# A scan kernel with its stores of y issued by SP in place of ACT, and the copies of C spread over three units

## The reference, cut to what matters

```
def step(state, inp):
    d, b, c, uu = inp
    dA = jnp.exp(d[..., None] * A_neg[:, None, :, :])
    state = dA * state + (d * uu)[..., None] * b[:, :, None, :]
    y = jnp.einsum('kbcn,kbn->kbc', state, c)
    return (state, y)
```

## Time and profile before

| | |
|---|---|
| median of 3 runs | 16748.27 us (16746.03 to 16751.82) |
| the profiled execution | 16740.79 us |
| its span | 16739.1 us |
| scan pass of layer 2 in it | about 8542 to 15095 us |
| granted clock of TensorE, mean | 0.856 |

### The profile page before, as it was taken

The page is one execution under the profiler, slowest core; times in us unless marked ns, Lnnn a source line. Parts: engine busy times, 40 slices in busy tenths (PEclk is TensorE's granted clock), DMA queues, the critical chain, the costliest instruction groups (busy, mean ns, idle before and its releaser), DMA issues. The chain is left out here.

```text
span 16739.1 us, 371849 instructions
## 1 busy us (share of the span) xinstructions
PE 13258.6 (79%) x130080; PEld 8791.3 (53%) x130080; DVE 11153.8 (67%) x10439; ACT 8476.8 (51%) x15113; POOL 6761.1 (40%) x3199
## 2 busy tenths in 40 slices
PE   7889999899988965444657887888778878887799
PEld 5666666666666642221235555555455545554477
DVE  5666666666666655554568887888788878885532
ACT  4444444444444435445556666666666666662200
POOL 1000000000000003234368888888888888881100
PEclk9999999999999988776768888888888888886799
DMA  5222222222222226668599999999999998997611
GB/s 128 58 68 57 57 60 55 61 60 56 58 65 61 55 86 159 157 163 201 147 210 208 207 208 206 206 208 208 206 207 208 207 205 207 208 209 211 184 44 37
DMA packets 1861415, 2344.84 MB, mean 140 GB/s; under 512 B 1067492, under 2 KB 1757932, under 8 KB 1836012
## 3 DMA queue, kind: packets, MB, share of 16 engines
q1 hardware_dynamic: 1606124, 2120.92, 53.4%
q10 hardware_dynamic: 242816, 134.91, 4.0%
q0 software_dynamic: 12288, 86.71, 2.3%
HBM read 1814.60 MB, written 556.32 MB: 142 GB/s over the span
## 5 line engine op out<-in xcount | busy, mean ns | idle before, releaser
L1789 DVE TENSOR_TENSOR_SCAN L2.h<-L2.ps,L2.db 128x912 f32<-128x912 f32 x2688 | 5400.7, 2046 | 1181.3 <-ACT L2.db L1712 1068.1
L1601 POOL TENSOR_TENSOR L2.db<-L2.du,L2.bt 128x896 f32<-128x896 f32 x2688 | 5560.1, 2097 | 1068.7 <-ACT L2.du L1719 832.6
L1623 PE MATMUL L2.ps<-L2.dm,L2.wa 32*128 32x112 f32 x21504 | 2441.9, 326 | 503.4 <-DVE L2.h L1789 383.7
L1705 ACT ACTIVATE L2.ps<-L2.ps 128x896 f32<-128x896 f32 x2688 | 2440.9, 908 | 492.0 <-PE L2.ps L1623 440.3
L1645 PE MATMUL L2.ps<-L2.h,L2.cd 128*8 128x96 f32 x50176 | 2576.8, 362 | 79.9 <-ACT L2.ysum L1726 67.1
L1623 PEld LDWEIGHTS L2.ps<-L2.dm,L2.wa 32*128 32x128 f32 x21504 | 1898.5, 220 | 1306.4 <-DVE L2.h L1789 785.6
L1635 PE MATMUL L2.ps<-L2.few,L2.fan 8*128 8x448 f32 x2688 | 1603.3, 680 | 832.9 <-ACT L2.du L1719 826.7
L1645 PEld LDWEIGHTS L2.ps<-L2.h,L2.cd 128*8 128x8 f32 x50176 | 1435.6, 108 | 806.3 <-ACT L2.ysum L1726 236.1
L1726 ACT COPY L2.ysum<-L2.ps 128x384 f32<-128x384 f32 x1568 | 751.7, 479 | 771.1 <-PE L2.ps L1645 666.5
L314 POOL TENSOR_TENSOR L1.x_res<-L1.x_res,L1.ob 96x3136 f32 (+1 forms) x16 | 95.4, 5977 | 2583.9 <-ACT L1.qv L457 2583.9
L1635 PEld LDWEIGHTS L2.ps<-L2.few,L2.fan 8*128 8x128 f32 x2688 | 443.5, 205 | 1192.4 <-ACT L2.du L1719 861.7
(11 more groups left out here) (258 smaller groups left out, 21196.1 us busy)
## 6 DMA issues: line engine op xcount, KB each, us to landing
L2.du<-du SPq DMA_DIRECT2D x4032, 224.0 KB, 6.0
L2.dm<-d SPq DMA_DIRECT2D x896, 336.0 KB, 7.2
y<-L2.ysum ACTq DMA_DIRECT2D x896, 84.0 KB
L0.left<-table SPq DMA_DIRECT2D x48, 1176.0 KB
L0.right<-table SPq DMA_DIRECT2D x48, 1176.0 KB
L1.left<-table SPq DMA_DIRECT2D x48, 1176.0 KB
L1.right<-table SPq DMA_DIRECT2D x48, 1176.0 KB
du<-L2p.work SPq DMA_DIRECT2D x64, 784.0 KB, 7.8
```

Of the source, the lines that this page charges most:

```text
L1601: pool.tensor_tensor(db[:, n % RB, :, 2:ROW], du[:, n % RD, :].rearrange("p (c t) -> p c t", t=SPAN), row, ALU.mult)\
L1623: mm = pe.matmul(decays[n % RA][:, lo:lo + SPAN], wa[rows, u * QUAD + e, :], dm[rows, u * QUAD + e, :], start=True, stop=True)
L1705: act.activation(a, a, ACT.Exp).then_inc(a_ready, 1)
L1789: dve.tensor_tensor_scan(h[:, half, u * UNIT:(u + 1) * UNIT, :].rearrange("p c t -> p (c t)"), decays[n % RA], db[:, n % RB, :, :].rearran ...
```

## The change

The four stores of a half-span's sums are no longer issued by ACT at the end of the half-span in which they are taken. SP issues them in the half-span after that: two in its unit 5 and two in its unit 6, behind the du loads of the same unit. At its unit 5 SP waits for `sum_out`, the count of takes, first. The wait of ACT at the first take, for `y_stored[half]`, keeps its place and its count; the counts of the semaphore come from the same four stores. After the last half-span SP stores the last two halves. The eight copies of C are made in lots of 3, 3 and 2 after units 11, 12 and 13 in place of all eight after unit 11 and the stores; their two waits stand before the first lot.

```
--- before.py
+++ after.py
@@ -1524,8 +1524,18 @@
                                   ap=[list(rows.ap[0]), [0, STATES // COPIES], list(rows.ap[1])])
                     sp.dma_start(du[:, slot, g * QUAD * SPAN:(g + 1) * QUAD * SPAN], src).then_inc(du_in[slot], 16)
 
-            def half_span(k, s, half, later, table):
-
+            def store_y(k, s, half, quarters):
+                for q in quarters:
+                    at = s * SPAN + SPAN // 4 * q
+                    if k % 2:
+                        at = at * -1 + (TOK - SPAN // 4)
+                    rows = slice(at, at + SPAN // 4) if isinstance(s, int) else bass.ds(at, SPAN // 4)
+                    place = y_dram[k, :, rows, half * HALF:(half + 1) * HALF]
+                    sp.dma_start(place, ysum[32 * q:32 * q + BATCH, :, :]).then_inc(y_stored[half], 16)
+
+            def half_span(k, s, half, earlier, later, table):
+
+                fills = count(sp, k, s, 2 * FILLS, (half - 1) * FILLS)
                 units = count(sp, k, s, 2 * UNITS, half * UNITS)
                 for u in range(UNITS):
                     sp.wait_ge(b_ready, units + (u + 1))
@@ -1541,6 +1551,11 @@
                             sp.wait_ge(cd_made, made)
                         steady(sp)
                         load_cc(k, s)
+                    if 5 <= u <= 6 and earlier is not None:
+                        if u == 5:
+                            sp.wait_ge(sum_out, fills + 2)
+                            steady(sp)
+                        store_y(*earlier, half, range(2 * (u - 5), 2 * (u - 5) + 2))
                     if u == 4 and table is not None:
                         sp.wait_ge(d_ready, count(sp, k, s, 4 * UNITS, half * 2 * UNITS))
                         load_wa(table, 1 - half)
@@ -1560,8 +1575,12 @@
                     later = (k + 1, 0) if k + 1 < DIRS else None
                 else:
                     later = (k, s + 1) if isinstance(s, int) else (k, sp.snap(s + 1))
-                half_span(k, s, 0, (k, s), k if k and isinstance(s, int) and s == 0 else None)
-                half_span(k, s, 1, later, k + 1 if last and k + 1 < DIRS else None)
+                if isinstance(s, int) and s == 0:
+                    earlier = (k - 1, NSPANS - 1) if k else None
+                else:
+                    earlier = (k, s - 1) if isinstance(s, int) else (k, sp.snap(s - 1))
+                half_span(k, s, 0, earlier, (k, s), k if k and isinstance(s, int) and s == 0 else None)
+                half_span(k, s, 1, earlier, later, k + 1 if last and k + 1 < DIRS else None)
 
             sp.wait_ge(cleared, 1)
             sp.dma_start(image[:], ap["c_image"]).then_inc(image_in, 16)
@@ -1576,6 +1595,9 @@
                 with sp.Fori(1, NSPANS - 1) as s:
                     span(k, s, False)
                 span(k, NSPANS - 1, True)
+            for half in range(2):
+                sp.wait_ge(sum_out, (DIRS * HALVES - 1 + half) * FILLS + 2)
+                store_y(DIRS - 1, NSPANS - 1, half, range(4))
             for half in range(2):
                 sp.wait_ge(y_stored[half], 64 * DIRS * NSPANS + 64)
 
@@ -1682,20 +1704,12 @@
             act.wait_ge(cleared, 1)
             act.wait_ge(image_in, 32)
 
-            def store_y(k, s, half):
-                for q in range(4):
-                    at = s * SPAN + SPAN // 4 * q
-                    if k % 2:
-                        at = at * -1 + (TOK - SPAN // 4)
-                    rows = slice(at, at + SPAN // 4) if isinstance(s, int) else bass.ds(at, SPAN // 4)
-                    place = y_dram[k, :, rows, half * HALF:(half + 1) * HALF]
-                    act.dma_start(place, ysum[32 * q:32 * q + BATCH, :, :]).then_inc(y_stored[half], 16)
-
-            def make_cd(k, s, fills):
-
-                act.wait_ge(cc_in, count(act, k, s, 16, 16))
-                act.wait_ge(sum_ready, fills + 2 * FILLS)
-                for b in range(BATCH):
+            def make_cd(k, s, fills, batches):
+
+                if batches[0] == 0:
+                    act.wait_ge(cc_in, count(act, k, s, 16, 16))
+                    act.wait_ge(sum_ready, fills + FILLS)
+                for b in batches:
                     act.activation(cd[:, b, :], cc[:], ACT.Identity, scale=image[:, b:b + 1]).then_inc(cd_made, 1)
 
             def decay(n, spreads):
@@ -1744,17 +1758,9 @@
                         copy_du(n // 4, n % 4 - 1, units, copies)
                     decay(n, spreads)
                     carry(half, u, units, begun)
-                if not first:
-                    act.wait_ge(sum_out, before + (FILLS + 2))
-                    steady(act)
-                    if half:
-                        store_y(k, s, 0)
-                    elif begun:
-                        store_y(k - 1, NSPANS - 1, 1)
-                    else:
-                        store_y(k, act.snap(s - 1), 1)
-                if half == 0:
-                    make_cd(k, s, before)
+                    if UNITS - 1 <= n <= UNITS + 1:
+                        at = 3 * (n - UNITS + 1)
+                        make_cd(k, s, count(act, k, s, 2 * FILLS), range(at, min(at + 3, BATCH)))
 
             for k in range(DIRS):
                 half_span(k, 0, 0, k == 0, True)
@@ -1765,8 +1771,6 @@
             act.wait_ge(y_stored[0], 64 * DIRS * NSPANS + 64)
             for f in range(FILLS):
                 take_sum(DIRS - 1, 1, f, (DIRS * HALVES - 1) * FILLS)
-            act.wait_ge(sum_out, DIRS * HALVES * FILLS + 2)
-            store_y(DIRS - 1, NSPANS - 1, 1)
 
         @block.vector
         def _(dve):
```

## The result

The changed kernel takes 17,702.7 us (median of 4 runs, 17,687.7 to 17,722.5), the kernel before 16,749.9 (4 runs): ratio 1.057, 95% interval 1.0552 to 1.0588. It is 953 us slower; forecast were 1,055 us, within 517 to 1,704. The profiled execution has a span of 17,686.0 us.

What follows compares the result with a forecast made beforehand. No engine was full; ACT's order of work set the pace. Per span 2 x 14.5 - 20.58 = +8.4 us, with the clock +9.4, x 112 = +1055 on 16,748.3: 17,800 us, between 17,265 and 18,450.

Steps and rivals of the forecast that it cites:

- take 0: First of seven copies from PSUM into ysum, in unit 4; ACT forecast to wait there some 220 times, 2 to 7 us.
- D: Stretch from Pool 11 to take 0, while SP issues and lands stores; 14.5 us a half, 12.6 to 17.
- the edit on the copies: Copies of C in lots over units 11 to 13, in time for the first sum in unit 15; costed at nothing.
- take 6: Last of the seven copies into ysum, unit 10; stretch from take 0 forecast within a microsecond of 14.5 and 15.5.
- Pool 11: End of GpSimd's unit 11 of a half, for which SP waits at its units 4 and 5.
- The issues ahead of the stores: SP's bt, dm and du issues and wait on sum_out between Pool 11 and the first store: 3.6 us.
- The two du loads in series: Unit 6's loads between second and third store, taken in series with the stores in SP's queue: 1.8 us.
- the lower bound 12.6: Least D: 3.6 us of issues ahead plus 9.0 us for the four stores nearly alone.
- The clock: TensorE idling before take 0 carries the low clock into the chain of sums: 1.0 us a span, 0 to 1.8.
- The first, stores landing in time: Rival: stores land before ACT needs them, decided at D = 10.3 us; faster, 16,130 us; chance 0.06.
- the second rival: Stores wait behind loads in SP's queue, SP issues du loads of units 8 to 10 late: 18,900 us; chance 0.08.
- ACT's relief: ACT freed of issuing the stores; claimed to be covered by the wait at take 0 and to bring nothing.

Runs made afterwards that it cites:

- e3: The changed kernel with all four stores in SP's unit 5, no du loads between them: 17,306.0 us.
- e11: The changed kernel, still one ysum, with SP's stores one each in units 5, 6, 7 and 8: 17,868.5 us.
- e4: The changed kernel with all four stores in SP's unit 4, behind its du loads and ahead of bt and dm: 16,873.6 us.
- e5: The changed kernel with two ysum, one for each half, SP's order of issues kept: 16,519.8 us.
- e2: The changed kernel with all eight copies of C after unit 11 instead of in lots: 17,710.5 us.
- e1: The kernel before with the copies of C in lots of 3, 3, 2, stores staying on ACT: 16,582.6 us.
- e6: Against the kernel before: two ysum, copies in lots, stores on ACT, one after each of units 0 to 3 of the next half: 16,181.0 us.
- e9: The kernel before with a second ysum and nothing else: 16,716.9 us.

## Why the prediction was right

**The mechanism.** It held at each step that the profile was to show: 222 waits at take 0 (220 forecast), no idle at unit 12, one of 4.6 us before unit 4, D alike in both halves (13.9 in the mean), no second wait for du in this kernel (GpSimd waits 106 us for du in the pass after, 212 before, by its waits), and the edit on the copies hidden. Cutting the span at take 0, take 6 and Pool 11 made it a sum of chains, and the change touched one of them directly. Two signs failed. Take 0 to take 6 stayed within a microsecond of its old time in half 1 (15.0 us in the mean, 14.5 before) but not in half 0 (17.0, 15.6 before). And SP's stores are not held 1 to 2 us each: their issue takes 0.30 us in the median, and the time shows at the loads behind them.

**D.** Predicted 14.5, measured 13.9 a half (27.8 / 2). The issues ahead of the stores were right to 0.1 us. The two du loads in series cost 1.4 us a half (e3 against the changed kernel) and not 1.8; the lower bound 12.6 was met by e3, which has no loads between, with 24.9 / 2 = 12.5. Against before that is +6.6 us a span by the means, in place of +8.4. Of the difference 0.6 is that the mean of before is 21.2, while the one span that I read had 20.58.

**The clock.** Predicted 1.0 us a span, measured +2.0 in take 0 to take 6 (32.0 against 30.0). That term was too small, since I counted one slow unit a half. In the span shown it is three in half 0: at 11018 to 11022 the granted clock is 0.50, 1.2 GHz, and the spread matmuls take 1.10 us (timeline of TensorE, after); by 11028 they are back at 0.65. In half 1 of the same span the clock is back at 1.00 by 11055, 4 us after take 0.

```profile
11025.65 1.10 PE L1645 MATMUL L2.ps<-L2.dm,L2.wa 32*128 32x112 f32 x8
...
11028.26 0.65 PE L1645 MATMUL L2.ps<-L2.dm,L2.wa 32*128 32x112 f32 x8
```

The spread of the spans agrees with that (65.0 to 68.6 us, 5 to 95% of them, with D varying by under 1 us). The trace also separates the clock from the wait before it. Take the 110 stretches take 0 to take 6 of half 0 (half-spans 3 to 222) and sort them by their mean granted clock; the last column is the longest idle of TensorE in the 12 us up to take 0:

```
granted clock    stretches   take 0 to take 6   D ahead   TensorE idle ahead
0.90 to 0.97        44            15.5 us        13.7 us        5.7 us
0.75 to 0.90        17            17.5           14.7           6.7
under 0.75          49            18.2           13.8           5.9
```

The first and the last row have nearly the same wait, yet the first takes no longer than before (15.6) and the last 2.6 us more. So the wait alone costs nothing behind take 0; the low clock does. e11 says the same: its wait is longer (D 15.3), its clock in these stretches higher (0.90 against 0.84), and take 0 to take 6 only 0.7 us above before. Why the clock comes back early in some spans and late in others stays open.

**The sum.** +6.6 + 2.0 = 8.5 us a span by unrounded values (forecast 9.4), x 112 = 952 against 953 measured. That these agree is no test, since the columns cover the whole span. That the forecast came within 102 us is in part luck: the D part was 1.8 us a span too high and the clock 1.0 too low, and these offset each other.

**The rivals.** The first, stores landing in time, was refuted. Its point of decision, D = 10.3, was right for the wait alone, and incomplete: e4 has D = 9.4 and is still slower, for the loads behind its stores. In this the second rival was half right: SP, held by the stores, does issue the loads behind them late. In the changed kernel those of units 8 to 10 are issued 6.6 to 7.1 us after their slot is free (1.8 to 4.1 before), but they still land 3.9 to 5.1 us ahead of their use, because VectorE is stopped at unit 4; GpSimd pays for it where loads are issued later still (e3, those of unit 6 at 6.3 us in place of 2.5) and where VectorE is hardly stopped or not at all (e4, e5). I had also written that ACT's relief is covered by the wait; in the changed kernel the lots are (e2). Outside it they are worth 167 us (e1), and with the stores apart some 400 more (e1 to e6, in which the second ysum, nearly nothing in e9, has its share in letting them be apart).

## What to carry to other kernels

When a store is moved to another issuer, look first at who reuses its source, and measure from the earliest moment at which the new issuer may issue to that reuse; with one buffer, four stores begun some 5 us later (3.5 after Pool 11 in place of 1.6 before) cost 953 us, with two buffers the same change won 230, and with one store a unit 570 (against e9, which has two buffers and the old order, 197 and 537). Put stores like these apart in a queue, since a row of four was paid by whatever was issued next, on either engine; no run varies their size or their rows. A part that gains alone may gain nothing in company (the lots: 167 us, 0 and 0 in three settings), so time each edit where it is to stand.

## What the runs showed of the hardware that was not expected

A store of 8 partitions with rows of 384 bytes is cheap to issue and dear to have issued. One line's instructions of e6, one store a unit on ACT (ns, min/median/max), beside 842 median for four in a row:

```profile
L1692 ACTq DMA_DIRECT2D y<-L2.ysum x896: 282/283/2007, 8592.7 to 14542.6; - x180
```

In the changed kernel the issues of the stores themselves are short too, 0.30 us in the median, and the time appears at the du loads after them: 3.24 us for two. In a list by line such a cost stands under the wrong name.
